# Graph attention in two layers on one core: fewer signals from TensorE, and a shorter memset in front of every gather

## The reference

```python
edge_index = jnp.stack([src, dst])            # 53125 edges, sorted by dst; 3125 nodes of 128 features
h = jnp.maximum(_layernorm(x, axis=-1), 0.0)
x = x + _L0_gnn_ref(h, ...)                   # 8 heads of 16
h = jnp.maximum(_layernorm(x, axis=-1), 0.0)
x = x + _L1_gnn_ref(h, edge_index, edge_attr_32, ...)

# layer 0                                     # layer 1
e = leaky(a_src[src] + a_dst[dst])            # score = <q[dst], k[src]> / 4 + edge_attr @ We + be
p = exp(e - segment_max(e, dst)[dst])         # exp_s = exp(score - segment_max(score, dst)[dst])
alpha = p / segment_sum(p, dst)[dst]          # attn = exp_s / (segment_sum(exp_s, dst)[dst] + 1e-8)
out = segment_sum(alpha * h[src], dst) + bias # out = segment_sum(attn * v[src], dst) @ Wo + bo
                                              # then the residual and a layer norm with gamma, beta
```

## Time and profile before

| | |
|---|---|
| median of three runs | 1507.73 us |
| the profiled execution's own time | 1507.14 us |
| its span, first to last instruction | 1505.4 us |
| mean granted TensorE clock | 0.687 of full speed |
| busy: POOL, PE, DVE, ACT | 1213.3, 954.2, 931.1, 635.1 us |
| gathers (line 493) | 880, mean 988 ns |
| memsets in front of them (line 479) | 880, mean 365 ns |

### The profile page before, as it was taken

How to read it: one execution, slowest core, us unless ns; L and a number is a source line. 1 busy time by engine, 2 the same in 40 slices (tenths; PEclk the granted TensorE clock), 3 DMA queues, 4 the chain that set the end, 5 groups by cost and what they waited for, 6 DMA issues and landing times.

```text
span 1505.4 us, 21963 instructions
## 1 busy us (share of the span) xinstructions
PE 954.2 (63%) x4985; PEld 801.6 (53%) x4985; DVE 931.1 (62%) x3002; ACT 635.1 (42%) x1699; POOL 1213.3 (81%) x1806
## 2 busy tenths in 40 slices
PE   5546575756657575755575667576666667676775
PEld 4335464545545454634454566465555556575654
DVE  6446565665656565656753666566666666666668
ACT  5624344343434343442168244434434444434404
POOL 5888888888888888886038888888888888888820
PEclk9656655666555666566597687777878777776765
DMA  6222222221222222222133333333333333333211
GB/s 140 70 68 47 68 47 67 47 68 47 67 47 69 47 66 47 62 46 82 49 107 88 87 89 88 88 88 88 89 88 90 88 88 88 88 88 88 86 31 43
DMA packets 54209, 110.41 MB, mean 73 GB/s; under 512 B 16876, under 2 KB 30848, under 8 KB 53956
## 3 DMA queue, kind: packets, MB, share of 16 engines
q0 software_dynamic: 36288, 91.12, 23.2%
q1 hardware_dynamic: 16483, 17.39, 4.2%
q10 hardware_dynamic: 1313, 0.50, 0.1%
HBM read 100.60 MB, written 8.81 MB: 73 GB/s over the span
## 4 chain that ended last, share of the span: by engine, by line
POOL 38%; issue 6%; DVE 5%; PE 3%; ACT 1%; DMA 0%; DVEq 0%; POOLq 0%; SPq 0%; ACTq 0%
POOL G L493 28%; POOL pad_i L479 10%; PE bank L826 2%; DVE halves L1048 1%; DVE acc L1402 1%; DVE mv L1055 0%; DVE G L1542 0%; DVE hn L1550 0%; DVE xs L1496 0%; DVE hn L1495 0%; DVE hn L1494 0%; PE bank L873 0%; ACT hn L547 0%; DVE G L1539 0%; DVE hn L1493 0%
## 5 line engine op out<-in xcount | busy, mean ns | idle before, releaser
L493 POOL DMA_INDIRECT G<-table,idx_all x880 | 869.0, 988 | 143.1 <-issue 120.2
L826 PE MATMUL bank<-PV,S 128*125 128x144 f32 x1760 | 435.4, 406 | 105.2 <-DVE PV L1379 83.6
L826 PEld LDWEIGHTS bank<-PV,S 128*125 128x125 f32 x1760 | 361.9, 279 | 134.1 <-issue 120.2
L1402 DVE TENSOR_TENSOR acc<-acc,bank 125x144 f32 x880 | 260.5, 296 | 175.7 <-PE bank L826 113.8
L479 POOL MEMSET pad_i<- 1x332 int32 x880 | 321.5, 365 | 17.6 <-DMA table<-h0b 8.8
L597 ACT ACTIVATE S<-iota_n,lid 128x125 f32<-128x125 f32 x880 | 275.7, 386 | 0.7 <-DVE pen L1143 0.7
L810 PE MATMUL bank<-qe,ST 125*128 x880 | 150.3, 325 | 57.7 <-DVE prod L1199 41.8
L810 PEld LDWEIGHTS bank<-qe,ST 125*128 125x128 f32 x880 | 132.4, 230 | 67.4 <-issue 66.5
L1379 DVE TENSOR_TENSOR PV<-G,PV 128x512 f32<-128x512 f32 x220 | 150.8, 686 | 18.9 <-issue 18.8
L601 ACT ACTIVATE S<-S,ones 128x500 f32<-128x500 f32 x220 | 156.6, 712 | 7.2
L607 ACT ACTIVATE ST<-bank 125x512 f32<-125x512 f32 x110 | 66.8, 607 | 218.8 <-PE bank L797 141.7
(11 more groups left out here) (220 smaller groups left out, 1241.7 us busy)
## 6 DMA issues: line engine op xcount, KB each, us to landing
G<-table,idx_all POOLq DMA_INDIRECT x880
prod<-in_edge_attr_dram SPq DMA_DIRECT2D x8, 672.0 KB
table<-G SPq DMA_DIRECT2D x12, 224.0 KB
bias_rows<-qe SPq DMA_DIRECT2D x1, 1664.0 KB, 5.8
table<-h0b SPq DMA_DIRECT2D x8, 178.5 KB
out_dram<-G SPq DMA_DIRECT2D x8, 168.0 KB
prod<-in_edge_attr_dram SPq DMA_DIRECT2D x8, 90.0 KB
xs<-in_x_dram SPq DMA_DIRECT2D x1, 504.0 KB
```

What stands on the lines that cost most here:

```text
L493: pool.indirect_dma_start(G[:, u, v, 0:w], None, table, bass.IndirectOffsetOnAxis(ap=idx_all[:, g * GV + v:g * GV + v + 1], axis=0)).then_ ...
L826: last = pe.matmul(sums_bank(p)[0:BN, at:at + H * SLOT], S[:, ur, v, :], PV[:, v, :, :].rearrange("p h k -> p (h k)"), start=True, stop=True)
L1402: ve.tensor_tensor(a, a, o, ALU.add).then_inc(s.sem["acc_added"], 1)
```

## The change

Four kinds of edit.

1. `space(332)` becomes `space(300)`.
2. PE gives fewer signals. `sums` no longer signals after batches 0 and 1 (except in the last group). `t_done` is raised after quarters 1 and 3 alone (and after quarter 2 of group 0 in layer 1). `expanded` is raised in the first two groups of each layer alone. `pT` is gone.
3. Who waited for a signal that is gone waits for a later one of the same engine: `node_rows(0)` and `node_rows(2)` for the signal of the second of two `spread_ids`; `evac(0)` for that of the second transpose, `evac(2)` for `hop2`; a wait on `expanded` for the signal of the batch of `sums` that PE does next; a wait on `pT` for `al_mm`; `add(0)` for `hop1` and `add(3)` for `hop2` in place of the batches' own signals.
4. On DVE `visit_scans` stands ahead of `add(0)` instead of behind it.

```diff
+NS = NB - 2                                     # NB = 6 batches
@@ gathers
-                            space(332)
+                            space(300)
@@ new helpers
+        def sums_done(r, p):
+            if r == GROUPS - 1:
+                return NS * r + p + 1
+            return 0 if r < 0 else NS * r + max(p - 1, 1)
+        def wait_expanded(eng, n, g, j):
+            if g < 2:
+                wait(eng, L[n]["expanded"], 4 * g + j + 1)
+            else:
+                wait(eng, L[n]["mm_done"], sums_done(g - 2, (2, 3 if n else 2, 4, 4)[j]))
+        def transposed(n, g, j):
+            return 2 * g + 1 + j // 2 + (n if g or j > 2 else 0)
@@ ScalarE
-                    wait(act, s["t_done"], 4 * g + j + 1)
-                    wait(act, s["expanded"], 4 * (g - 1) + j + 1)
+                    if j == 2 and g:
+                        wait(act, s["hop2"], g)
+                    else:
+                        wait(act, s["t_done"], transposed(1, g, j))
+                    wait_expanded(act, 1, g - 1, j)
...
-                        wait(act, s["pT"], q + 1)
-                        wait(act, s["mm_done"], NB * q)
+                        wait(act, s["al_mm"], q + 1)
+                        wait(act, s["mm_done"], sums_done(q - 1, NB - 1))
@@ TensorE
-                              start=True, stop=True).then_inc(s.sem["t_done"], 1)
+                    if j % 2:
+                        last.then_inc(s.sem["t_done"], 1)
...
-                    last.then_inc(s.sem["t_done"], 1)
+                    if j % 2 or (j == 2 and g == 0):
+                        last.then_inc(s.sem["t_done"], 1)
...
-                    last.then_inc(s.sem["expanded"], 1)
+                    if g < 2:
+                        last.then_inc(s.sem["expanded"], 1)
...
-                    last.then_inc(s.sem["mm_done"], 1)
+                    if p > 1 or r == GROUPS - 1:
+                        last.then_inc(s.sem["mm_done"], 1)
...
-                        pe.transpose(sT[:, 2 * P:3 * P], EP[:, 0, :], ident[:, :]).then_inc(s.sem["pT"], 1)
+                        pe.transpose(sT[:, 2 * P:3 * P], EP[:, 0, :], ident[:, :])
@@ VectorE
-                        wait(ve, s["t_done"], 4 * g + j + 1)
-                        wait(ve, s["expanded"], 4 * (g - 1) + j + 1)
+                        wait(ve, s["t_done"], transposed(0, g, j))
+                        wait_expanded(ve, 0, g - 1, j)
...
-                        if v == lo:
-                            wait(ve, s["mm_done"], NB * r + BATCH_OF[v] + 1)
+                        if v == lo and BATCH_OF[v] == 0 and mid:
+                            wait(ve, s["hop1"], q + 1)
+                        elif v == lo and BATCH_OF[v] == 1 and mid:
+                            wait(ve, s["hop2"], q + 1)
+                        elif v == lo:
+                            wait(ve, s["mm_done"], sums_done(r, BATCH_OF[v]))
...
                     node_rows(2)
+                    visit_scans()
                     add(0)
-                    visit_scans()
                     add(1)
```

More of the change, by code:

```diff
@@ L365, in load_ids @@
             def load_ids(g, u):
-                wait(sp, L[0]["t_done"], 4 * (g - UNROLL + 1))
+                wait(sp, L[0]["t_done"], transposed(0, g - UNROLL, 3))
                 sp.dma_start(lid_ring[32 * u:32 * u + 1, :],
@@ L632, in step @@
                         wait(act, s["dd_ready"], q + 1)
-                        wait(act, s["pT"], q)
+                        wait(act, s["al_mm"], q)
                         act.activation(EP[:, 0:k, :], DD[:, 0:k, :], ACT.Exp).then_inc(s.sem["p_ready"], 1)
@@ L789, in spread_ids @@
                         wait(pe, a_Te, attr_done(g - 1))
-                    pe.matmul(tp[j % 2][0:BN, :], ones_b[32 * u:32 * u + 1, :], lid_ring[32 * u:32 * u + 1, j * QV * P:(j + 1) * QV * P],
-                              start=True, stop=True).then_inc(s.sem["t_done"], 1)
+                    last = pe.matmul(tp[j % 2][0:BN, :], ones_b[32 * u:32 * u + 1, :],
+                                     lid_ring[32 * u:32 * u + 1, j * QV * P:(j + 1) * QV * P], start=True, stop=True)
+                    if j % 2:
+                        last.then_inc(s.sem["t_done"], 1)
                 def one_hot_T(g, u, j):
@@ L1196, in qk_product @@
                         ve.wait_ge(s_gath[u][j], gathered(n, u, j, i))
-                        wait(ve, s["expanded"], 4 * g + j + 1)
+                        wait_expanded(ve, 1, g, j)
                         wait(ve, s["score_parts"], 4 * g + j - 1)
@@ L1214, in part_sum @@
                             return
-                        wait(ve, s["expanded"], 4 * g + min(2 * half + 2, new))
+                        wait_expanded(ve, 0, g, 2 * half + 1)
                         wait(ve, s["scoreT"], g)
@@ L1367, in loop_weights @@
                         wait(ve, s["p_ready"], q + 1)
-                        wait(ve, s["pT"], q)
+                        wait(ve, s["al_mm"], q)
                         ve.scalar_tensor_tensor(PS[:, :], p0, 0.0, EP[:, 1, :], op0=ALU.is_lt, op1=ALU.mult).then_inc(s.sem["ps_ready"], 1)
@@ L1375, in weigh @@
                         wait(ve, s["pcols"], r + 1)
-                        wait(ve, s["mm_done"], NB * r)
+                        wait(ve, s["mm_done"], sums_done(r - 1, NB - 1))
                         c0 = F if n else 0
```

10 lines of the change are left out of this document (5 added, 5 removed).

## The result

The changed kernel takes 1487.07 us (median of four, 1486.06 to 1487.43); the kernel before, run beside it, 1504.81 us (1501.74 to 1507.80, four runs). The ratio is 0.9888, with an interval of 0.9873 to 0.9904: 1.1% faster. Forecast were 1482 us, between 1470 and 1494. The profiled execution took 1486.06 us, 21.1 less than the one before.

What follows compares the result with a forecast made beforehand. GpSimd's row of gathers and memsets was taken to bound the kernel. 1507.1 - 23.5 (memset) - 5.5 (layer 0's stalls) + 4.5 (layer 1's stalls) = 1482.6, stated as 1482 us, range 1470 to 1494.

Steps and rivals of the forecast that it cites:

- What bounds: GpSimd's row of gathers, memsets and gaps, 1333.6 us or 89% of the span; what is taken from it shortens the time.
- The memset: On GpSimd, 32 columns less save 26.7 ns in each of 880 memsets: -23.5 us.
- The signals at nothing: Fewer PE signals and later waits reach no gather, since GpSimd waits for `pv_ready` alone with time to spare: 0 us.
- DVE's waits for `G`, smaller by 0.4 us a group in both layers: DVE's waiting for gathers to land, 7.2 and 2.4 us a group in layers 0 and 1, shrinks by about 0.4.
- Layer 0's stalls, -5.5: The seventh gather's 0.47 us stall goes, one of about 0.3 us comes further on: -5.5 us, between -9 and 0.
- the formula: A gather waits for the end of a two-SBUF-input DVE operation begun before it, if that ends 0.125 us past its start.
- Layer 1's stalls, +4.5: `weigh(2)` moves 0.2 to 0.3 us later and stalls the seventh gather 0.2 to 0.35 us: +4.5 us, between -3 and +9.
- The rest of the program, 0: Setup, the stretch between the layers and the end have no gathers in them and stay as they were.
- That the stalls fall away: Rival: both layers' steps fall between the gathers, stalls shrink from 31 to about 17 us, time 1469 us; chance 12%.
- That layer 1 is bound by the step: Rival: layer 1 no longer waits for gathers and keeps its time, only layer 0 gains: 1491 to 1496 us; chance 6%.
- That the space does nothing: Rival: memset a fixed cost, or gathers cannot be issued sooner than 1.48 us after the last: 1506 us; chance 4%.
- Twice stalled in every group: Rival: `weigh(2)` and `weigh(3)` both start just ahead of a gather in both layers, 63 us of stalls: 1516 us; chance 3%.

Runs made afterwards that it cites:

- e5: Changed kernel with each `weigh` replaced by a `tensor_reduce` with one SBUF input, leaving out the softmax weights; 1458.66 us, ratio 0.972.
- e7: Changed kernel with memsets of 200 columns; 1407.97 us, ratio 0.938 to the kernel before.
- e2: Changed kernel with the old memset of 332 columns, so signals, waits and DVE's order alone are changed; 1498.8 us, ratio 0.997.
- e3: Kernel before with `visit_scans` ahead of `add(0)` on DVE and nothing else changed; 1494.05 us, ratio 0.994.
- e8: Kernel before, all its signals kept, with `visit_scans` ahead of `add(0)` and memsets of 200 columns; 1402.5 us, ratio 0.934.
- e9: Changed kernel run once more without any edit; 1488.11 us in one run.
- e1: Kernel before with memsets of 300 columns and nothing else changed; 1487.66 us, ratio 0.990.
- e6: Changed kernel with memsets of 232 columns; 1455.1 us, ratio 0.970 to the kernel before.
- e12: e6 with `OHF` moved ahead of the two `DD` operations on DVE, with a wait for `al_mm`; 1633.66 us, ratio 1.090.
- e11: e8 with `add(6)` moved between `OHF` and `weigh(3)` on DVE; 1406.05 us, ratio 0.936.

## Why the prediction was right, and where it was off

**What bounds: right.** GpSimd's row sets the time. e5 took 27 us of stalls out of it and the time fell by 28; e7 took 83 ns from each memset, 73 us, and 7 us of stalls, and the time fell by 79.

**The memset: right.** 27.7 ns measured against 26.7 taken, 24.4 us against 23.5.

**The signals at nothing: right.** GpSimd never waited for `pv_ready`, and in both pairs that differ by the signals and their waits (e2 and e3, e7 and e8) the kernel with fewer was not faster.

**DVE's waits for `G`, smaller by 0.4 us a group in both layers: not so.** They went from 193.9 and 64.9 us to 99.3 and 66.9 in the first profile and to 177.8 and 120.9 in e9. Only layer 0 in e9 is near the forecast, 16 us less where 11 were taken. Before and the first profile of after are executions in which TensorE's signals came late (see the last section), and DVE waits for PE there in place of `G`; e2 and e3, which keep the old memset and have one late signal each, waited 111 and 118 us in layer 1. So the margin of 2.4 us a group that the prediction read there was smaller than the kernel's in an undisturbed execution. The forecast hangs on there being a margin, not on its size.

**Layer 0's stalls, -5.5: the number right in the first profile (-5.3), half right in kind.** The seventh gather's 0.47 us is gone, as forecast (20 such stalls before, 9.3 us together, and 3 after, 0.6 us). The 0.3 us at the eleventh is not there in the first profile: two eleventh gathers were stalled, by 0.31 and 0.63 us, and the rest is spread over nearly all places of the group, 4.1 us of it in six stalls behind `OHF`. In e9 it has come, in twelve groups, but there nine stalls of 0.6 us behind `OHF`, which the formula did not know, bring layer 0 to 15.3 us, only 2.4 less than before. That the first profile gave -5.3 is luck as far as what was added goes.

**Layer 1's stalls, +4.5: the right place, too small.** The step that was mis-sized is "everything up to `weigh(2)` moves by 0.2 to 0.3 us". It moved 0.44 us. The scans begin 0.55 us after `RH` in both kernels; before, `add(0)` ran in that gap, and now it stands behind them, so that from the scans to `weigh(2)` it takes 1.31 us in place of 0.87. So the stall at the seventh gather is 0.41 us and not 0.2 to 0.35, and layer 1 got +6.9 (e9: +5.7).

**The rest of the program, 0: off by 1.7 us.** Outside the two rows of gathers the execution was 1.7 us longer, most of it (1.3) between the layers; in e9 the row of layer 1 begins 76.0 us after the end of that of layer 0, against 74.9 before. It was not looked into.

In sum 1482.6 - 0.9 (memset) + 0.2 (stalls, layer 0) + 2.4 (stalls, layer 1) + 1.7 (the rest) = 1486.0, the profiled execution's 1486.1.

**The rivals.** That the stalls fall away: their sum went from 28.6 to 30.3 us. That layer 1 is bound by the step: refuted by e7 and e8, which are 79 and 85 us faster. That the space does nothing: refuted by e1. Twice stalled in every group: layer 1 came to 0.65 us a group, short of the 0.99 at which the change would have turned slower. e6 with 46 us, 0.84 a group, came nearer.

## What to carry to other kernels

Where one engine's queue sets the time, price a change by what it does to that queue, instruction by instruction, and let the rest wait; then ask which other engine can hold up single instructions of it. On this kernel a DVE operation with two inputs in SBUF, or a row of such operations without a gap, costs a gather up to 0.77 us, and whether it hits depends on tenths of a microsecond. The stalls of e1, e3 and e6 came out 11, 10 and 20 us off what was expected: a stall term should carry a range of that size either way, and a version should be chosen by running several near ones. To be rid of the term, let the long operation read from PSUM or have one input, as e5 did for a price in function.

## What the runs showed of the hardware that was not expected

**Signals of TensorE that come late.** The trace has each change of a semaphore as an event. In eleven of the fourteen traces the event of nearly every signal of TensorE stands about 15 ns behind the end of its matmul; at most 8 of 666 or 1159 come more than 0.1 us later. In three traces it is otherwise: before (356 of 1159 later than 0.1 us), the first one of after (334 of 666) and e12 (376 of 666); some events are missing there (before has 949 for 1159 signals), as if two signals had come at once, so a delay is counted to the next event. Medians of the late ones are 1.5 to 3.1 us. With the gathers in front, before and after lost little by it: 1507.1 us in that execution of before, against 1497.4 to 1506.9 in its 33 executions beside the experiments, and 1486.1 of after against 1488.1 in e9. But e12 is some 180 us slower than e6, in all four of its executions, while the kernel before ran at 1501.6 us beside it. Whether the chip, the program or both decide it is open: e1 to e8 ran on one chip, e9 to e11 on a second, e12 on a third, and e12's kernel was not tried on the other two. It also leaves open what fewer signals are worth on a chip in that state with a shorter memset; e7 and e8 were compared on one without late signals. The Trainium skill, "VectorE: DVE Perf Modes", section "The TRN2 errata — SBUF-src ops pay a fixed extra latency per instruction", warns that semaphore increments at a high rate from one engine can deadlock another; no run here shows whether that is what these traces show.

**TensorE's clock.** The granted clock was 0.67 of full speed in the first profile of after and 0.70 in e9, with the same program. The time differed by 2 us.
